# The sublayer weight's load is issued behind the last context instead of between two gate weight chunks

## The reference

```
q, k, v = layernorm(x) Wq^T + bq,  ctx Wk^T + bk,  ctx Wv^T + bv     # 16 heads of 32
q' = relu(q Wqf^T);  k' = relu(k Wkf^T) * mask                       # 64 features a head
kv = sum over tokens of k' v;   k_sum = sum over tokens of k'
x  = x + (q' kv / (q' k_sum + 1e-8)) Wo^T + bo

h  = act_quant(layernorm(x))          # rounded to 127 steps of each row's maximum
W  = weight_quant(w) = clip(round(w * s), -1, 1) / s,  s = 1 / mean|w|
g, u = h Wg^T, h Wu^T                 # 512 -> 2048
a  = u * relu(g)^2
a  = a * rsqrt(mean(a^2) + 1e-6) * sublayer_weight
x  = x + act_quant(a) Wd^T            # 2048 -> 512
```

## Time and profile before

| | us |
|---|---|
| median of 3 runs | 424.59 (424.51 to 425.42) |
| profiled execution, its own time | 425.54 |
| its span | 423.7 |
| TensorE (PE) busy | 409.8, 97% |
| VectorE (DVE) busy | 338.8, 80% |
| ScalarE (ACT) busy | 290.3, 69% |
| GpSimd (POOL) busy | 152.6, 36% |

### The profile page before, as it was taken

How to read it: one execution, slowest core, us unless ns; L and a number is a source line. 1 busy time by engine, 2 the same in 40 slices (tenths; PEclk the granted TensorE clock), 3 DMA queues, 4 the chain that set the end, 5 groups by cost and what they waited for, 6 DMA issues and landing times.

```text
span 423.7 us, 11313 instructions
## 1 busy us (share of the span) xinstructions
PE 409.8 (97%) x4822; PEld 284.4 (67%) x4851; DVE 338.8 (80%) x501; ACT 290.3 (69%) x409; POOL 152.6 (36%) x291
## 2 busy tenths in 40 slices
PE   8999999999999999999999999999999999999986
PEld 7888889988978847644944674584575576464333
DVE  4554849479459999999996998897999698897993
ACT  4666989892274397687479649578772958939970
POOL 0000000006015653652565246455349034547640
PEclk9999999999999999999999999999999999999999
DMA  7993656550050300331212033033031021421346
GB/s 248 419 374 107 252 201 235 215 196 9 5 224 3 113 15 0 63 73 41 51 50 52 25 64 88 25 63 90 1 76 37 14 51 31 95 51 24 59 99 166
DMA packets 51170, 42.42 MB, mean 100 GB/s; under 512 B 43056, under 2 KB 44080, under 8 KB 49200
## 3 DMA queue, kind: packets, MB, share of 16 engines
q1 hardware_dynamic: 51120, 41.70, 32.3%
HBM read 27.01 MB, written 4.19 MB: 74 GB/s over the span
## 4 chain that ended last, share of the span: by engine, by line
PE 38%; DVE 30%; issue 8%; ACT 8%; POOL 7%; DMA 5%; SPq 2%; DVEq 0%; POOLq 0%
PE ps L408 8%; PE ps L539 7%; PE ps L556 6%; DVE zb L977 5%; PE ps L358 4%; PE ps L360 3%; PE ps L359 3%; DMA xs<-in_wq_dram 3%; DVE tk L988 3%; DVE zb L984 2%; POOL zb L1192 2%; ACT rb L722 2%; DMA xs<-in_wg_dram 2%; PE ps L515 2%; PE ps L430 2%
## 5 line engine op out<-in xcount | busy, mean ns | idle before, releaser
L539 PE MATMUL ps<-tu,xqT 128*128 128x512 bf16 x248 | 59.0, 379 | 2.3 <-DVE zb L977 1.2
L539 PE MATMUL ps<-tg,xqT 128*128 128x512 bf16 x242 | 57.8, 379 | 2.1 <-issue 1.3
L556 PE MATMUL ps<-td,yqT 128*128 128x512 bf16 x202 | 46.1, 379 | 2.3 <-DVE zbe L977 1.2
L539 PEld LDWEIGHTS ps<-tu,xqT 128*128 128x128 bf16 x256 | 23.9, 98 | 32.6 <-issue 2.6
L539 PEld LDWEIGHTS ps<-tg,xqT 128*128 128x128 bf16 x256 | 23.8, 98 | 31.0 <-issue 4.5
L977 DVE TENSOR_TENSOR zb<-ps,rb 128x1024 f32<-128x1024 f32 x29 | 35.3, 1218 | 9.4 <-ACT rb L718 8.9
L722 ACT ACTIVATE rb<-zb 128x1024 f32<-128x1024 f32 x29 | 30.6, 1054 | 17.1 <-DVE zb L977 16.9
L988 DVE TENSOR_REDUCE tk<-zb 128x1 f32<-128x1024 f32 x30 | 36.2, 1209 | 3.2 <-POOL zb L1192 3.0
L1192 POOL TENSOR_TENSOR zb<-zb,g_b 128x1024 f32<-128x1024 f32 x11 | 27.2, 2472 | 29.2 <-ACT rb L722 26.4
L556 PEld LDWEIGHTS ps<-td,yqT 128*128 128x128 bf16 x208 | 19.7, 98 | 26.8 <-DVE zbe L977 1.7
L358 PE MATMUL ps<-aph,wqh 128*128 128x256 f32 x128 | 36.8, 287 | 0.0
(11 more groups left out here) (154 smaller groups left out, 1046.1 us busy)
## 6 DMA issues: line engine op xcount, KB each, us to landing
xs<-in_wg_dram SPq DMA_DIRECT2D x4, 1024.0 KB, 14.2
xs<-in_wu_dram SPq DMA_DIRECT2D x4, 1024.0 KB, 5.6
xs<-in_wd_dram SPq DMA_DIRECT2D x4, 1024.0 KB, 7.6
xs<-in_x_dram SPq DMA_DIRECT2D x8, 512.0 KB, 4.2
out_dram<-xs SPq DMA_DIRECT2D x15, 256.0 KB, 2.2
craw<-in_ctx_dram SPq DMA_DIRECT2D x7, 512.0 KB, 5.5
xs<-in_wk_dram SPq DMA_DIRECT2D x4, 256.0 KB, 4.5
xs<-in_wv_dram SPq DMA_DIRECT2D x4, 256.0 KB, 5.9
```

Of the source, the lines that this page charges most:

```text
L539: k = pe.matmul(ps[:, b0 + n, :], xqT[:, i % 3, kc, :], tern[w][:, o:o + 512], start=kc == 0, stop=kc == KC - 1)
L556: k = pe.matmul(ps[:, D_BANK[i], :], yqT(i)[:, j, :], tern[2][:, 512 * j:512 * j + 512], start=j == 0, stop=j == 15)
```

## The change

One call is moved in SyncE's list. It stood between the loads of the gate matrix's first two chunks, and now stands behind the loads of contexts 6 and 7 and ahead of the first chunk of the down matrix. Nothing else is changed.

```
             load_context(1, 0); load_feature_weights(); load_value_bias(); load_query_weights(); load_ffn_weights(0, 0)
-            load_sublayer_weight(); load_ffn_weights(0, 1); load_context(2, 0); load_ffn_weights(0, 2); load_context(3, 0)
+            load_ffn_weights(0, 1); load_context(2, 0); load_ffn_weights(0, 2); load_context(3, 0)
             load_ffn_weights(0, 3); load_context(4, 0); load_context(5, 0)
             for n in range(4):
                 load_ffn_weights(1, n)
-            load_context(6, 0); load_context(7, 0)
+            load_context(6, 0); load_context(7, 0); load_sublayer_weight()
             for n in range(4):
                 load_ffn_weights(2, n)
```

## The result

The changed kernel takes 426.57 us (median of 15 runs, 425.32 to 428.69) against 424.92 us for the kernel before (15 runs, 424.49 to 426.74). The ratio is 1.0033, with a 95% interval of 1.0019 to 1.0047: it is slower by 1.4 us (1.65 between the medians), where 1.0 us less was forecast. The profiled execution took 427.82 us, 1.25 above the median, with a span of 426.0. TensorE's busy time is the same to 0.1 us; what grew is its idle time.

The account below looks back on a forecast made before the run. TensorE, busy 97% of the span, was taken to bound the kernel through its in-order queue. Gains of 0.90 + 0.10 = 1.0 us, with the new place at 0, gave 424.59 - 1.0 = 423.6 us, range 423.1 to 424.9.

Parts of the forecast that it names:

- (a): Between gate chunks 0 and 1: removing the transfer lands chunk 1 2.5 us earlier, ending line 430's 0.90 us stall.
- (b): At the second key-value product, near 40 us: 0 to 0.15 us more is gained, taken as 0.10.
- (c): In SyncE's queue: the moved issue, 0.48 us, fits in 3.2 us of idle time and adds no wait.
- (d): New place, about 65 to 70 us: down weights 0.7 us late, hidden by 1.15 us to spare; cost 0.
- The slower rival: Late down chunks stall TensorE before the third total near 85 us, up to 1.35 us; 424.9 to 425.9; chance 0.12.

Follow-up runs that it names:

- the third of before: The kernel before, unedited, profiled a third time; that execution took 426.29 us.
- the second profile: The kernel before, unedited, profiled a second time; that execution took 423.73 us.
- experiment 1: The changed kernel with the sublayer weight loaded behind the output weights instead of ahead of the down weights; 425.53 us, ratio to before 0.9992.
- experiment 2: The kernel before plus a second load of the same sublayer weight in the new place, behind context 7; 427.66 us, ratio 1.0049.
- experiment 12: The changed kernel with the sublayer weight held until the first half of the fifth context's keys is done on TensorE; 427.12 us, ratio to before 1.0050.
- Experiment 4: As experiment 1, with context 4's load also held until the first key-value product is done; 425.10 us, ratio to before 0.9982.
- 7: As Experiment 4, but with the sublayer weight in four quarters issued at about 104, 107, 111 and 114 us; 425.27 us, ratio to before 0.9994.
- 9: As Experiment 4, with 13 more warming matmuls ahead of everything; ratio to before 0.9990.
- experiment 5: The changed kernel with only half the sublayer weight in the new place, the rest loaded behind the output weights; 425.59 us, ratio to before 0.9993.
- experiment 6: The changed kernel with some of the fourth context's key-feature matmuls issued twice, adding 104 matmuls where 52 were meant; 437.21 us, ratio to before 1.0264.
- experiment 13: The changed kernel, unedited, profiled a second time; that execution took 427.07 us.

## Why the prediction was wrong

- **"The second chunk lands 2.5 us earlier" (a): right.** Its magnitudes started between 22.61 and 23.46 in six profiles, forecast 24.0, against 26.54; the copies ended before 30, forecast 30.7.
- **"The cover is 1.7 us, so the whole 0.90 us goes" (a): wrong.** Two things were amiss. The 0.90 us came from one execution, and others have 0 to 0.32 of the wait. And behind it stood a second wait, for the instruction block of line 430, that ends near 34.2 in the first profile of the changed kernel and in the third of before, whether the copies are early or late. In the very profile that the prediction was read from, this block's packet ended at 32.44 and TensorE passed the place at 33.74, 1.30 us later, as it does at the stalls: with the copies on time the block would, by this estimate, still have held TensorE at matmul 47 until about 33.7. The 0.11 us inside the stage, which I put down to the second copy, is probably this block as well; the second profile, without the copies' wait, has the stage just as long (32.33 to 33.98). What the removal is worth was measured as 0.3 us, with an interval from a loss of 0.3 to a gain of 0.9 (experiment 1).
- **"0.10 us more" (b):** not separable from the above. The second key-value product, forecast near 39.7, starts at 39.30 to 41.04 us (mean 40.03) in the seven profiles with the removal and no hold of context 4, and at 39.82 to 41.32 (mean 40.73) in the five with the early part of the kernel before. So something like 0.7 us may be gained up to there, which so few profiles that differ by 1.5 us among themselves can't settle.
- **SyncE's queue (c): right.** The issue took 0.43 us of idle time there.
- **"A delay of 0.7 us is hidden, and costs TensorE nothing" (d): wrong, and this decided the sign.** The down weights' last magnitudes were 0.55 us late (0.7 forecast), and the total had its cover. What was not priced is the other user of those DMA engines: TensorE's instruction block asked for at about 66.6 us. Its term was 0 in the sum and measured 1.54 and 1.86 us in the two profiles (in the second another 1.6 us at the lower clock), 1.7 us by the ratio to experiment 1 and 2.1 by experiment 2. The gap of 2 us in the DMA share at 67 to 69 us, which I read as room, was what let this block through.
- **The slower rival had the place, the sign and nearly the time** (424.9 to 425.9), by another mechanism: it laid the loss at line 457, where no wait ever appeared. Its chain is real, as experiment 12 shows, but is met first at line 449 with 0.45 us to spare. In the changed kernel the 1.54 us of stall give that chain the time that it lacks, so the two prices don't add.
- The clue was on the page before: q8 in the list of DMA queues, and a wait of 0.28 us named "issue" at 19.5 us, in the middle of line 430 under full DMA load. Neither found its way into the sum.

Open remains why the early stalls come and go between executions of one kernel, why the loads at 90 to 95 us delay a block in some kernels (0.25, 0.77, 1.13 and 0.24 us in experiments 1, 4, 7 and 9) and not in the profiles of before, when the clock falls behind a stall and when not, and the rest of experiment 12. Experiment 4 is the one version that came out faster than both kernels, 0.9982 (0.9972 to 0.9993), 0.75 us; two near relatives of it (7 and 9) don't confirm it, so I take it as the place to look and not as a settled gain.

## What to carry to other kernels

A gap in the DMA engines' load isn't free room when an engine streams through its instructions quickly: count its instructions from a break in blocks, find where the next block is asked for, and let no bulk load be queued just ahead of that. A wait named "issue" in the middle of a run of equal instructions is the sign of it. A stall of under 1 us should be looked for in two or three profiles before it is worth a change, and for a transfer that is moved, every wait that its neighbours' users gate needs its cover counted, not only the last in the chain.

## What the runs showed of the hardware that I had not expected

- TensorE's instructions come in blocks of 256 over the DMA engines that carry the data (38 packets of 16 KB), and a block can be late by what is queued ahead: 1.07 us less stall for 0.5 MB less (experiment 5). In the five full stalls of line 449 TensorE went on 1.26 to 1.38 us after the block's packet had ended.
- A block that is run through in 1.33 us under full DMA load cost 4.28 us of idle time (experiment 6). After it TensorE's granted clock was 0.72 in the mean from 76 to 82 us, which is time at the lower of its two levels (1.2 and 2.4 GHz), and the distance between value matmuls grew from 0.23 to 0.43 us. After the stall of 1.86 us it was 0.59 from 72 to 76 us (experiment 13); after that of 1.54 us it stayed at 1.00.
- Thirteen matmuls more in the warming, which took 0.7 us longer with the same number of columns, made the kernel before 1.0 us slower (1.0023, 1.0003 to 1.0043), with all operations and transfers behind it unchanged; at most 0.3 us of that was left at the first key features, and its two breaks of 0.67 us lie at block boundaries.
